# Perceiver block on one core: where the inner tiles' normed rows, second residual rows and next inputs stand in the order of the sync queue

## The reference, cut to what matters

```python
x = x + xattn(layernorm(x), ctx)          # 64 x 32 x 512 queries, 64 x 257 x 512 keys = values, 16 heads
x = x + attn(layernorm(x), ...)           # 16 heads over 32 rows, rotated queries and keys
x = x + ffn(layernorm(x), ...)            # 8 experts, each row goes through the one with the largest gate
```

## Time and profile before

| what | value |
|---|---|
| median of 3 runs | 780.48 us (776.76 to 782.8) |
| the profiled execution | 774.74 us, its span 772.9 us |
| granted TensorE clock of that execution | 0.982 |
| PE busy | 703.4 us, 91% of the span |
| DVE, ACT, POOL busy | 75%, 55%, 43% |
| DMA traffic | 129.07 MB, 167 GB/s over the span |

### The profile page before, as it was taken

How to read it: one execution, slowest core, us unless ns; L and a number is a source line. 1 busy time by engine, 2 the same in 40 slices (tenths; PEclk the granted TensorE clock), 3 DMA queues, 4 the chain that set the end, 5 groups by cost and what they waited for, 6 DMA issues and landing times. The chain is left out here.

```text
span 772.9 us, 26293 instructions
## 1 busy us (share of the span) xinstructions
PE 703.4 (91%) x10502; PEld 549.4 (71%) x10502; DVE 582.7 (75%) x1184; ACT 428.8 (55%) x1085; POOL 335.2 (43%) x687
## 2 busy tenths in 40 slices
PE   5898989998999999989999899999977889999997
PEld 4555868787787777867978778778765556666664
DVE  4378678886988878878888798886465757788883
ACT  3345466674766656657667565674223546555652
POOL 1112454443354435343444344434225256866542
PEclk9899999999999999999999999999998999999999
DMA  9995545655557456565565555632414996544420
GB/s 253 306 231 120 155 132 158 178 150 143 167 155 192 143 158 178 139 180 152 166 180 151 148 172 159 186 111 71 178 42 137 357 393 229 172 152 144 143 98 5
DMA packets 114377, 129.07 MB, mean 167 GB/s; under 512 B 14478, under 2 KB 81294, under 8 KB 114256
## 3 DMA queue, kind: packets, MB, share of 16 engines
q1 hardware_dynamic: 108192, 111.12, 49.3%
q0 software_dynamic: 5520, 16.26, 6.1%
q10 hardware_dynamic: 544, 0.00, 0.0%
HBM read 114.77 MB, written 14.42 MB: 167 GB/s over the span
## 5 line engine op out<-in xcount | busy, mean ns | idle before, releaser
L924 ACT ACTIVATE prob<-scores,negmax 128x257 f32<-128x257 f32 x256 | 118.1, 475 | 106.3 <-DVE negmax L1124 103.4
L1379 POOL COPY plast<-prob 128x2 f32<-128x2 f32 x128 | 23.9, 188 | 203.8 <-ACT prob L924 202.3
L564 PE MATMUL stage_banks<-qkv_hi,operand_hi 128*128 128x398 f32 x256 | 99.2, 387 | 0.0
L565 PE MATMUL stage_banks<-qkv_lo,operand_hi 128*128 128x398 f32 x256 | 87.9, 343 | 1.8 <-issue 1.8
L1124 DVE TENSOR_REDUCE negmax<-scores 128x2 f32<-128x514 f32 x128 | 82.5, 686 | 8.3 <-PE scores L632 8.2
L566 PE MATMUL stage_banks<-qkv_hi,operand_lo 128*128 128x398 f32 x256 | 88.1, 344 | 0.0
L1114 DVE STREAM_TRANSPOSE k_t<-keys 128x512 f32<-128x512 f32 x128 | 82.6, 684 | 2.8 <-DMA keys<-in_ctx 2.8
L1676 PE MATMUL stage_banks<-w_all,hidden 128*128 x184 | 82.8, 592 | 0.6 <-ACT hidden L1729 0.6
L642 PE MATMUL scores<-consts,prob 128*128 128x128 f32 x512 | 78.2, 277 | 0.9 <-issue 0.4
L1772 DVE TENSOR_TENSOR w_lo<-w_all,w_hi 128x512 fp32r<-128x512 f32 x89 | 74.3, 892 | 0.2
L1119 DVE COPY prob_t<-scores 128x512 f32<-128x512 f32 x64 | 43.1, 673 | 35.3 <-PE scores L642 35.2
(11 more groups left out here) (262 smaller groups left out, 1655.6 us busy)
## 6 DMA issues: line engine op xcount, KB each, us to landing
keys<-in_ctx SPq DMA_DIRECT2D x256, 128.0 KB
context<-in_ctx SPq DMA_DIRECT2D x64, 512.0 KB, 4.3
w_all<-in_L_ffn_W SPq DMA_DIRECT2D x16, 1024.0 KB, 13.3
b<-in_L_ffn_b SPq DMA_DIRECT2D x23, 256.0 KB, 3.5
norm_scratch<-norm SPq DMA_DIRECT2D x16, 256.0 KB, 3.2
x_tile<-in_x SPq DMA_DIRECT2D x8, 256.0 KB, 2.9
x_pair<-in_x SPq DMA_DIRECT2D x8, 256.0 KB, 2.9
x_scratch<-x_tile SPq DMA_DIRECT2D x8, 256.0 KB, 2.2
```

The lines of the kernel that those rows point to most:

```text
L564: pe.matmul(to, op_hi[op][:, c, :], w_hi[name][:, c, columns], start=(c == 0), stop=False)
L565: pe.matmul(to, op_hi[op][:, c, :], w_lo[name][:, c, columns], start=False, stop=False)
L924: act.activation(prob[pair][:, gg, :], scores[:, g, 0:J], ACT.Exp, bias=negmax[b % 2][:, g:g + 1], accum_out=sums[t % 2][:, g, bl:bl + 1]) ...
```

## The change

On SP, the load of the next tile's input moves from block step 16 to block step 24, and in the loop it now stands behind `load_context` and `load_keys` of its step. For tiles 0 to 13 the store of x2 moves from offset 100 to 104 and the store of the normed rows from 104 to 111. That puts the second store at k = 1, behind the next batch's keys (L521) and ahead of its context (k = 2). The last two tiles' stores stay where they are. The measure of the next input goes from block step 22 to 29 on DVE, its root from 28 to 30 on POOL, its scaling from 30 to 32 on ACT, and PE's turn of it from 35 to 36. No instruction is added or taken away.

```diff
-QUERIES, QUERIES_MOVE = -53, -50
-
-MEASURE_X, ROOT_X, SCALE_X = 22, 28, 30
+QUERIES, QUERIES_MOVE = -52, -50
+
+MEASURE_X, ROOT_X, SCALE_X = 29, 30, 32
...
+X_LOAD_AT, X2_STORE, NORM3_STORE = 2 * STEPS + 2, 104, 111
...
+        def stored_at(step, store, made, name):
+            inner, last = tile_at(step, store), tile_at(step, made, LATER[name])
+            return inner if 0 <= inner < T - 2 else last if last >= T - 2 else -1
+
         for step in range(LAST_STEP):
             b, k = divmod(step, STEPS)
             t, bl = divmod(b, BT)
-            if k == 5 and bl == 1 and t + 1 < T:
-                load_x(t + 1)
             if k == 2 and 1 <= b and b + 3 < B:
                 load_context(b + 3)
             if k == KEYS_LOAD_AT and 1 <= b and b + 2 < B:
                 load_keys(b + 2)
+            if k == X_LOAD_AT % STEPS and bl == X_LOAD_AT // STEPS and t + 1 < T:
+                load_x(t + 1)
...
-            t = tile_at(step, X2, LATER["X2"])
+            t = stored_at(step, X2_STORE, X2, "X2")
             if t >= 0:
                 until.wait_ge(x2_made, t + 1)
                 sp.dma_start(x2_dram[t * P:(t + 1) * P, :], x_tile[t % 4][:, :]).then_inc(x2_stored[t % 4], 16)
-            t = tile_at(step, SCALE3, LATER["SCALE3"])
+            t = stored_at(step, NORM3_STORE, SCALE3, "SCALE3")
             if t >= 0:
                 until.wait_ge(normed_r, t + 1)
                 sp.dma_start(norm3_dram[t * P:(t + 1) * P, :], norm3[:, :]).then_inc(norm3_stored, 16)
```

## The result

The changed kernel takes 832.02 us (median of 4 runs, 826.62 to 840.7) where the kernel before takes 780.62: a ratio of 1.0648, 95% interval 1.0596 to 1.07. It is slower, as forecast, and by 51 us where 33 were forecast; 832 lies above the range (785 to 828). The profiled execution took 834.13 us, its span 832.3.

A forecast was written before the change was run, and what follows sets the result against it. PE, busy 91%, bounds the kernel, so its waits count. The profiled 774.7 us plus 26 (12 blocks x 2.2) plus 9 in the set-up gives 810, set at 813 because the runs' median lies higher; range 785 to 828.

The forecast's parts named there:

- The mechanism, its place and its sign: Blocks 3 to 14: x lands late behind the context, DVE's measure waits, then PE; 2.2 us a block, 26 us slower.
- The second wait forecast on PE, the one for q: Steady blocks: PE gets q at 223.05 instead of 220.84, 2.2 us late, containing 1.4 us of waiting for bank 0.
- The room: Steady blocks: the measure must start by 215.9, DVE is ready at 215.76, so 0.13 us is left.
- The chain: Steady blocks: from start of x's measure on DVE to the end of POOL's L1412, which PE's turn of q needs, 4.95 us.
- The long wait in the set-up: Near 50 us: x(1) lands at about 60 behind a context, PE's unit 19 waits 8.9 us once, bounds 6 to 11.
- I take 218.1: Steady block: x, issued at 213.0 to 213.2 behind normed rows and context, lands at 218.1, bounds 215.9 to 218.5.
- Blocks 1 and 2 at nothing: In blocks 1 and 2 no normed rows are stored yet and DVE arrives later, so they cost nothing.
- I cost both at nothing by themselves: SP's two moved stores cost nothing by themselves, since contexts are loaded three batches ahead and keys a batch ahead.
- the 0.3 us that the landing had been given for the normed rows: Steady blocks: the normed rows' store ahead of x was given half its price of 0.65 us in x's landing.
- Rival 1: Steady blocks: x lands by 215.9, the chain fits by 0.1 us, only the set-up costs; 784 to 790 us; chance 0.15.
- Rival 3: SP doesn't go by steps, so steady blocks change under 0.5 us each; within 1%, 776 to 786 us; chance 0.12.
- Rival 2: Spreading SP's pile of DMAs ends PE's stops without a named wait; up to 8 us faster, 767 or 772; chance 0.07.

The follow-up runs named there:

- keys_held: The changed kernel, with SP waiting for x to land before issuing the keys of each block's last batch (blocks 1 to 14): 810.93 us, ratio 1.0405.
- measure_only: The kernel before with only the measure, root, scaling and turn of the next input moved, all DMAs at their old places: 778.5 us, ratio 1.0003.
- stores_only: The kernel before with both stores moved late and x loaded at block step 16, right behind the x2 store: 778.98 us, ratio 1.0012.
- old_stores: The changed kernel with both stores back at offsets 100 and 104, load of x and measure still late: 820.74 us, ratio 1.0517.
- early_x: The changed kernel with the load of x back at block step 16, right behind the x2 store: 781.01 us, ratio 1.0034.
- filler: The changed kernel plus seven small unread PE products per block (2 to 14) before the third quarter of qkv: 833.71 us, ratio 1.0652.
- x_behind_keys: The changed kernel with x loaded one step earlier, right behind its batch's keys, ahead of normed rows and context: 789.12 us, ratio 1.0112.

## Why the prediction was right and where it failed

Right:

- The mechanism, its place and its sign. x lands late, DVE's measure waits with L1185 behind it, PE waits for bank 0, and no engine computes more. The second wait forecast on PE, the one for q, comes only where the clock has stayed up (5 times, 2.7 us; in keys_held 11 times, 6.7 us); elsewhere PE comes to q late because it is slow.
- The room. 0.13 us was forecast as left over with the longer path, and measure_only costs nothing.
- The chain, 4.95 us from measure to turned part: 4.88 in the block shown. From measure to the turn of q it is 5.03 us in eleven of the twelve blocks of keys_held.
- The long wait in the set-up: 8.9 us forecast, 8.71 measured.

The step that failed is the time at which x lands, "I take 218.1, as the row with the same three in a row (keys, context, x) is nearest". The load of x was given what stands ahead of it in the queue, and nothing for what comes behind. In the pair of the earlier trace rows nothing came close behind. The next line of that queue in the kernel before is this:

```profile
113.59 2.55 SPq L463 DMA_DIRECT2D keys<-in_ctx  x4
```

This is 3.8 us after x was issued, when x had all but landed. In the changed order keys follow at once, which could have been read off: x at 213.1, and in the earlier trace rows the next keys are due at 214.32. The context was also further ahead there, 1.64 us, where it is 0.47 us ahead of x now. So the nearest row was near in its order and not in its surroundings. Per block, counted from the start of `stats_s`, forecast and then measured as the mean of the twelve: x is issued at +7.2 and +7.76; it lands 5.0 and 5.8 us after; the measure starts at +12.16 and +13.59. That is 1.43 us a block, 17 us, of which 0.6 us a block is the issue and 0.8 the landing. The issue had been read off one quick block: in the earlier trace rows the four keys take 2.55 us of SP, and in the mean of the twelve blocks of the same trace 2.86.

With the next keys held back x lands 1.3 us sooner and the measure starts at +12.31, nearly the forecast, and the blocks cost nearly the forecast sum. That they agree so well is luck in part: x is still issued 0.6 us later than forecast, and lands in 4.55 us in the mean instead of 5.0. That what comes behind x costs is shown by keys_held. That the held keys were the cause through the landing alone, and not also through what they free for the context, isn't separated. And keys close behind don't do it by themselves: in stores_only they were as close once, with nothing just ahead of x, and it landed in 2.7 us. What was under-priced is a load in the middle of a pile.

The other terms that were off:

- The clock. Nothing was given for it. With it the part from measure to turn of q is 5.47 us in the mean instead of 5.03, 12 x 0.44 = 5 us by position; and in the set-up 5.73 us instead of 3.5 for eight products, 2.2 us.
- Blocks 1 and 2 at nothing: 0.5 and 2.1 us. With the 11.5 us before the first `stats_s`, that is the 14.0 at the head of the program where 8.9 were forecast.
- "I cost both at nothing by themselves" is right for the stores (stores_only). In front of a late x they cost 0.5 us a block, and by old_stores that is SP's time of issue; the 0.3 us that the landing had been given for the normed rows doesn't show.
- One term helped. The twelve blocks of the kernel before are together 7.8 us longer than twelve clean ones, 5.9 of that in PE's three long stops without a named wait. Such stops now fall ahead of PE's wait for bank 0 and vanish in it. So 12 x 4.16 us (q turned at +19.06 instead of the clean +14.90) makes 49.9, less 7.8, plus 3.4 us in the other parts of the blocks: 45.5.

The rivals. Rival 1 (x in time, only the set-up costs) fell, as x lands at +13.6 in the mean where +10.0 (215.9) was needed. Rival 3 (SP doesn't go by steps) fell: x is issued behind that context in every one of the twelve blocks. Rival 2 fell in its cause and not just its sum: in early_x and stores_only x is in time and the pile is spread, and PE's stops stay, in all four kernels (before, after and these two) in blocks 4, 9 and 12, some 7 us behind the start of `stats_s`. What makes them isn't shown, but the traces have one more row on it, the queue on which a page of the profile lists instruction loads (84 packets of 16 KB, 85 in filler, where PE has more instructions):

```profile
q8 instruction: 84, 1.38, 0.8%
```

In the twelve blocks of the thirteen traces PE has 51 stops of 0.9 us or more without a named wait, and every one begins 0.2 to 1.6 us after a packet of that queue has started. Such packets come about every 7 us, and most pass without a stop. So the likely cause is that PE's next instructions weren't there yet, which no run here has tested; x, the stores and the keys have no part in it that shows.

## What to carry to other kernels

Before a load is moved in a queue, list what will be issued right behind it as well as ahead of it, with the distances in us, and take its landing only from a row where both sides are alike. Here the keys close behind made x land 1.3 us later, more than the store put in front (0.5 us), and less than all that stood ahead together (4.4 us of landing with nothing behind, 2.6 with nothing just ahead). A load that the next stage waits for goes ahead of large ones that are due three batches later: by x_behind_keys that alone was worth 39 of the 46 us in the blocks. And where a chain has 0.13 us of room, each further delay counts in full in every round, here with 0.4 us more for the low clock after the wait.

## What the runs showed of the hardware that was not expected

- How long a load takes to land depended on what was issued just ahead and just behind it, together. 256 KB took 2.6 us (median) with nothing of SP's in the 3.4 us or more ahead, though keys followed 0.5 to 2.0 us behind (early_x); 3.7 with keys ahead and normed rows and context behind (x_behind_keys); 4.4 with normed rows and context ahead and nothing behind until it had landed (keys_held); 5.8 with those ahead and four loads of keys 0.5 us behind. The Trainium skill (DMA: Bandwidth & Descriptors, Two DMAs through the same engine are not ordered) says that the descriptors of one queue start in order on a DMA engine but are pipelined, its read and write sides being separate queues. It doesn't say that those behind slow those ahead. The 1.4 us that keys_held took away leave room for it; no run here looks inside a DMA engine.
- The time that SP takes to issue is no constant. Four loads of keys took 2.55 to 3.83 us at one and the same place of the block, in the kernel before (up to 3.63) as in the others, and 4.37 in the set-up. That a full queue is the reason isn't shown: in keys_held they took 3.59 us just after x had landed, when the normed rows and the context ahead of it had landed too.
- After PE had stood 2.34 us and worked for about one, its clock fell to the 1.2 GHz level for 3 us. PE was busy 16.9 us longer in the twelve blocks, and by position only some 5 us of the time come from it.
